# Cross-attention: queries spread for four heads, maxima turned in a batch's banks, half batches between fourths of the projections

## What is computed

```python
x = x + _L0_xattn_ref(_layernorm(x), ctx_1024, ...)
...
q = split_heads(x_q @ Wq + bq) * dp_scale
k = split_heads(x_kv @ Wk + bk)
v = split_heads(x_kv @ Wv + bv)
attn = jnp.einsum('bhic,bhjc->bhij', q, k)
neg = -jnp.finfo(attn.dtype).max
attn = jnp.where(causal_mask, neg, attn)
attn = jax.nn.softmax(attn, axis=-1)
o = jnp.einsum('bhij,bhjc->bhic', attn, v)
```

## Time and profile before

| | us |
|---|---|
| runs (3) | 1687.93, 1688.18, 1692.31 |
| median | 1688.18 |
| the profiled execution | 1688.73 |
| its span, first to last instruction | 1686.9 |
| TensorE busy | 1578.0 |
| VectorE busy | 1045.9 |
| ScalarE busy | 964.8 |
| GpSimd busy | 697.7 |

### The profile page before, as it was taken

How to read it: one execution, slowest core, us unless ns; L and a number is a source line. 1 busy time by engine, 2 the same in 40 slices (tenths; PEclk the granted TensorE clock), 3 DMA queues, 4 the chain that set the end, 5 groups by cost and what they waited for, 6 DMA issues and landing times. The chain is left out here.

```text
span 1686.9 us, 48994 instructions
## 1 busy us (share of the span) xinstructions
PE 1578.0 (94%) x20162; PEld 1362.0 (81%) x20179; DVE 1045.9 (62%) x1445; ACT 964.8 (57%) x1848; POOL 697.7 (41%) x627
## 2 busy tenths in 40 slices
PE   6999999999887999999999987998799999999988
PEld 5888888888666889888898765986588898898863
DVE  7667777786346877777777343045676666666622
ACT  4677777777413466656656712352367777777742
POOL 5655555551004655554554000000375555555202
PEclk9999999999977999999999999999999999999998
DMA  7665555554234766555555352971475555555430
GB/s 180 166 198 131 120 140 131 132 123 106 65 116 116 183 182 170 143 145 138 137 147 126 88 207 85 362 256 51 127 175 140 138 128 120 140 133 132 100 108 4
DMA packets 149248, 235.65 MB, mean 140 GB/s; under 512 B 24200, under 2 KB 64516, under 8 KB 148100
## 3 DMA queue, kind: packets, MB, share of 16 engines
q1 hardware_dynamic: 141090, 225.29, 50.6%
q10 hardware_dynamic: 7938, 7.23, 1.7%
HBM read 107.26 MB, written 0.23 MB: 64 GB/s over the span
## 5 line engine op out<-in xcount | busy, mean ns | idle before, releaser
L1305 DVE TENSOR_REDUCE L_xattn_maxima<-L_xattn_ps 128x4 f32<-128x1024 f32 x588 | 691.6, 1219 | 327.3 <-PE L_xattn_ps L877 323.2
L1067 ACT ACTIVATE L_xattn_p_ring<-L_xattn_ps 128x512 f32<-128x512 f32 x1176 | 674.9, 599 | 340.8 <-PE L_xattn_ps L926 325.7
L926 PE MATMUL L_xattn_ps<-L_xattn_q_packed,L_xattn_k_packed 128*128 128x256 f32 x2352 | 452.1, 298 | 10.0 <-ACT L_xattn_p_ring L1067 5.0
L926 PEld LDWEIGHTS L_xattn_ps<-L_xattn_q_packed,L_xattn_k_packed 128*128 128x128 f32 x2352 | 335.3, 190 | 71.6 <-issue 35.9
L962 PE MATMUL L_xattn_ps<-L_xattn_p_ring,L_xattn_v_ring 128*17 128x128 f32 x9408 | 289.3, 273 | 1.0 <-ACT L_xattn_p_ring L1067 1.0
L962 PEld LDWEIGHTS L_xattn_ps<-L_xattn_p_ring,L_xattn_v_ring 128*17 128x17 f32 x9408 | 242.4, 97 | 23.6 <-ACT L_xattn_p_ring L1067 1.6
L845 PE MATMUL L_xattn_ps<-L_xattn_ctx_halves,L_xattn_w_halves 128*128 128x256 f32 x1764 | 260.9, 286 | 0.5 <-POOL L_xattn_ctx_halves L1224 0.4
L849 PE MATMUL L_xattn_ps<-L_xattn_w_halves,L_xattn_ctx_halves 128*128 128x256 f32 x1764 | 260.4, 286 | 0.0
L1239 POOL TENSOR_TENSOR L_xattn_k_ring<-L_xattn_k_full,consts 128x512 fp32r<-128x512 f32 x147 | 155.5, 1058 | 223.0 <-ACT L_xattn_k_full L1080 111.6
L1221 POOL TENSOR_TENSOR L_xattn_ctx_halves<-L_xattn_ctx_chunk,consts 128x512 fp32r<-128x512 f32 x129 | 134.4, 1042 | 263.1 <-DMA L_xattn_ctx_chunk<-in_ctx_chunks 178.9
L845 PEld LDWEIGHTS L_xattn_ps<-L_xattn_ctx_halves,L_xattn_w_halves 128*128 128x128 f32 x1764 | 233.3, 193 | 3.7 <-issue 1.8
(11 more groups left out here) (385 smaller groups left out, 1173.2 us busy)
## 6 DMA issues: line engine op xcount, KB each, us to landing
L_xattn_k_packed<-L_xattn_k_ring SPq DMA_DIRECT2D x588, 128.0 KB, 2.4
L_xattn_ctx_chunk<-in_ctx_chunks SPq DMA_DIRECT2D x147, 256.0 KB, 3.2
L_xattn_k_packed<-L_xattn_k_ring SPq DMA_DIRECT2D x588, 64.0 KB, 2.2
L_ffn_W<-in_experts_W SPq DMA_DIRECT2D x16, 1024.0 KB, 13.7
L_xattn_mask_chunk<-L_xattn_mask ACTq DMA_DIRECT2D x49, 128.0 KB, 3.0
weights<-in_pack_L_attn SPq DMA_DIRECT2D x10, 512.0 KB, 4.3
L_xattn_ctxT<-in_ctxT SPq DMA_DIRECT2D x5, 896.0 KB, 12.9
L_xattn_ctx<-in_ctx SPq DMA_DIRECT2D x5, 896.0 KB, 11.8
```

The lines of the kernel that those rows point to most:

```text
L926: last = pe.matmul(L.ps[:, bank, d * 2 * S:(d + 1) * 2 * S], self.k_packed[s][:, quarter, d, half * P:(half + 1) * P], q[:, 2 * pair:2 * p ...
L1067: act.activation(self.p[t % P_RING][:, 4 * quarter:4 * quarter + 4, :], L.ps[:, E_BANK[unit], :].rearrange("p (h n) -> p h n", n=S), ACT.Exp)\
L1305: dve.tensor_reduce(out[:, 4 * v:4 * v + 4], L.ps[:, M_BANK + 2 * v:M_BANK + 2 * v + 2, :] .rearrange("p b (k n) -> p (b k) n", k=2), AX_X ...
```

## The change

Three things change, all in `CrossAttention`.

1. `q_hi` and `q_pairs` hold four matrices instead of sixteen: for each half of the heads one that keeps the even and one that keeps the odd heads of width 16 (mask `pair16`). A strip of 32 rows still sees one head at a time. VectorE's two operations shrink from 1024 to 256 columns, ScalarE's low halves from 16 operations to 4 and its copy from 2048 to 512 columns. `pack_queries` reads from the smaller matrices; its number of transfers stays.
2. In steps 6 to 48 (`borrows`) the turned maxima go to bank 2 and the factors to bank 3, which belong to the batch of this step, once the first half of its first batch has been reduced. The second batch of the step waits until ScalarE has taken the factors. The units keep banks 0 and 1 for themselves. `pe_factor` moves three projection matmuls ahead, and on ScalarE `act_factor` goes ahead of the drain of the values.
3. In steps 1 to 4 each half of a batch stands before one fourth of the projections.

```diff
@@ -51,7 +51,7 @@
 QUANTIZED = "L0_ffn"
 PART = 1024
 CONSTS = [("identity", P), ("ones", P), ("causal", P), ("causal_T", P), ("rope_cos", S), ("rope_sin", S),
-          ("head16", 8), ("head32", 4), ("neg_half", 1), ("fill", P), ("turned", 1), ("turn_sign", 1)]
+          ("head16", 8), ("head32", 4), ("pair16", 2), ("neg_half", 1), ("fill", P), ("turned", 1), ("turn_sign", 1)]
 
 
 HELD_FOR = {"L0_attn": "L0_ffn", "L1_ffn": "L2_xattn"}
@@ -96,7 +96,7 @@
         "identity": np.eye(P), "ones": np.ones((P, P)), "fill": fill,
         "causal": np.where(p[None, :] > p[:, None], NEG, 0.0), "causal_T": np.where(p[:, None] > p[None, :], NEG, 0.0),
         "rope_cos": np.cos(angle), "rope_sin": np.sin(angle) * sign,
-        "head16": p[:, None] // 16 == np.arange(8)[None, :], "head32": p[:, None] // 32 == np.arange(4)[None, :],
+        "head16": p[:, None] // 16 == np.arange(8)[None, :], "pair16": p[:, None] // 16 % 2 == np.arange(2)[None, :], "head32": p[:, None] // 32 == np.arange(4)[None, :],
         "neg_half": np.full((P, 1), -0.5),
         "turned": (p % DH < 2)[:, None],
         "turn_sign": np.where(p % DH == 0, -1.0, np.where(p % DH == 1, 1.0, 0.0))[:, None],
@@ -574,11 +574,21 @@
     return 6 if step < NCHUNK else 8
 
 
+def borrows(step):
+
+    return LAG <= step < NCHUNK
+
+
 def e_order():
 
     at, bank, before, used = {}, [], [], {}
 
     def unit(key, step):
+        if key[0] != "scores" and borrows(step):
+            before.append(-1)
+            at[key] = len(at)
+            bank.append(M_BANK if key[0] == "turned" else M_BANK + 1)
+            return
         free = E_BANKS if step < NCHUNK else E_BANKS + (KV_BANK,) if step < NCHUNK + 2 else TAIL_BANKS
         b = min(free, key=lambda i: (used.get(i, -1), free.index(i)))
         before.append(used.get(b, -1))
@@ -614,7 +624,7 @@
         self.norm = NormRows(L, bank=ACC_BANK)
         sb = L.sb
         self.w_halves = [sb(f"w_halves{h}", [P, 2, DC, D], F32R) for h in range(2)]
-        self.q_hi = sb("q_hi", [P, H, S], F32R)
+        self.q_hi = sb("q_hi", [P, 2 * DC, S], F32R)
         self.q_packed = [sb(f"q_packed{c}", [P, H, S], F32R) for c in range(2)]
         self.ctx_chunk = [sb(f"ctx_chunk{c}", [P, DC, KEYS]) for c in range(3)]
         self.ctx_halves = [sb(f"ctx_halves{c}", [P, 2, DC, KEYS], F32R) for c in range(3)]
@@ -631,7 +641,7 @@
         self.stage_T = sb("stage_T", [P, S], F32R)
         self.factor = sb("factor", [P, 4 * S])
 
-        self.q_pairs = self.p_ring[:, 0:2, :, :]
+        self.q_pairs = self.p_ring[:, 0, :, :].rearrange("p (a h) n -> p a h n", h=2 * DC)[:, 0:2, :, :]
         flat = self.p[2].rearrange("p h n -> p (h n)")
         self.qT = flat[:, 0:DC * S].rearrange("p (c n) -> p c n", n=S)
         self.qT_halves = flat[:, DC * S:3 * DC * S].rearrange("p (a c n) -> p a c n", a=2, n=S)
@@ -731,10 +741,9 @@
             sp.wait_ge(L["q_lo_heads_ready"], DC)
             sp.wait_ge(L["q_copied"], 1)
         packed = self.q_packed[0][:, :, :].bitcast(F32)
-        sp.dma_start(heads(packed[0:32, :, :]), heads(self.q_pairs[own, 1, :, :])).then_inc(L["q_packed_ready"], 16)
-        sp.dma_start(heads(packed[32:96, :, :]), self.q_pairs[own, :, :, :]
-                     .rearrange("r a (c h) n -> r a c (h n)", c=DC)[:, :, :, 2 * quarter * S:(2 * quarter + 2) * S])\
-          .then_inc(L["q_packed_ready"], 16)
+        pairs = self.q_pairs[own, :, :, :].rearrange("r a (c k) n -> r a c (k n)", c=DC)
+        sp.dma_start(heads(packed[0:32, :, :]), pairs[:, 1, :, :]).then_inc(L["q_packed_ready"], 16)
+        sp.dma_start(heads(packed[32:96, :, :]), pairs).then_inc(L["q_packed_ready"], 16)
 
     def fill_queries(self, sp):
 
@@ -851,19 +860,24 @@
         if part % 2 and end == 6:
             last.then_inc(L["k_in_psum" if part == 1 else "v_in_psum"], 1)
 
-    def pe_batch(self, pe, step, d):
+    def pe_batch(self, pe, step, d, first=0, end=4):
 
         n = step - 1
         if not 0 <= n < NCHUNK:
             return
         L, batch, slot, bank = self.L, 2 * n + d, n % K_RING, self.L.ps[:, M_BANK:M_BANK + 4, :]
         cornered = self.causal and n == NCHUNK - 1
+        b = block_turned(step)
         pe.wait_ge(L["q_heads_ready"], d + 1)
-        if d == 0:
+        if d == 1 and b and borrows(step):
+            pe.wait_ge(L["e_drained"], E_AT["factor", b] + 1)
+        if d == 0 and first == 0:
             pe.wait_ge(L["k_hi_ready"], n + 1)
             if self.masked:
                 pe.wait_ge(L["fill_ready"], n + 1)
         for strips in ((0, 1), (2, 3)) if step < LAG else ((0, 1, 2, 3),):
+            if not first <= strips[0] < end:
+                continue
             if batch:
                 pe.wait_ge(L["batch_reduced"], 2 * (batch - 1) + strips[-1] // 2 + 1)
             if self.masked:
@@ -874,7 +888,7 @@
             for k in range(2):
                 for r in strips:
                     own = slice(32 * r, 32 * r + 32)
-                    last = pe.matmul(bank[:, r, k * KEYS:(k + 1) * KEYS], self.q_hi[own, 8 * d + 2 * r + k, :],
+                    last = pe.matmul(bank[:, r, k * KEYS:(k + 1) * KEYS], self.q_hi[own, 2 * d + k, :],
                                      self.k_ring[own, slot, 0, d, :], start=not self.masked, stop=not cornered,
                                      tile_position=(32 * r, 0), skip_group_check=True)
                     if k and r % 2 and not cornered:
@@ -931,17 +945,23 @@
 
     def pe_turned(self, pe, b):
 
-        L, unit = self.L, E_AT["turned", b]
+        L, unit, step = self.L, E_AT["turned", b], turn_step(b)
         pe.wait_ge(L["stage_ready"], b + 1)
-        self.pe_bank_free(pe, unit)
+        if borrows(step):
+            pe.wait_ge(L["batch_reduced"], 4 * (step - 1) + 1)
+        else:
+            self.pe_bank_free(pe, unit)
         pe.transpose(L.ps[0:64, E_BANK[unit], 0:S], self.stage[:, :], self.net.const("identity"))\
           .then_inc(L["e_filled"], 1)
 
     def pe_factor(self, pe, b):
 
-        L, unit = self.L, E_AT["factor", b]
+        L, unit, step = self.L, E_AT["factor", b], turn_step(b)
         pe.wait_ge(L["e_drained"], E_AT["turned", b] + 1)
-        self.pe_bank_free(pe, unit)
+        if borrows(step):
+            pe.wait_ge(L["batch_reduced"], 4 * (step - 1) + 1)
+        else:
+            self.pe_bank_free(pe, unit)
         for i in range(4):
             last = pe.matmul(L.ps[:, E_BANK[unit], i * S:(i + 1) * S],
                              self.net.spread[:, 4 * i:4 * i + 4, :].rearrange("p h n -> p (h n)"),
@@ -981,12 +1001,9 @@
                 pe.wait_ge(L["q_packed_ready"], 16 * (9 if self.masked else 8))
                 pe.wait_ge(L["v_ones_ready"], 1)
             if step < LAG - 1:
-                self.pe_batch(pe, step, 0)
-                self.pe_project(pe, step, 0)
-                self.pe_project(pe, step, 1)
-                self.pe_batch(pe, step, 1)
-                self.pe_project(pe, step, 2)
-                self.pe_project(pe, step, 3)
+                for part in range(4):
+                    self.pe_batch(pe, step, part // 2, part % 2 * 2, part % 2 * 2 + 2)
+                    self.pe_project(pe, step, part)
             elif step == LAG - 1:
                 self.pe_project(pe, step, 0)
                 self.pe_project(pe, step, 1)
@@ -1013,9 +1030,10 @@
                 if b is not None:
                     self.pe_turned(pe, b)
                 self.pe_unit(pe, m, 5)
-                self.pe_project(pe, step, 3)
+                self.pe_project(pe, step, 3, 0, 3)
                 if b:
                     self.pe_factor(pe, b)
+                self.pe_project(pe, step, 3, 3, 6)
                 self.pe_unit(pe, m, 6)
                 self.pe_batch(pe, step, 1)
                 self.pe_unit(pe, m, 7)
@@ -1149,9 +1167,9 @@
 
         L = self.L
         act.wait_ge(L["q_lo_ready"], 1)
-        for h in range(HPB):
-            last = act.activation(self.q_pairs[:, 0, c * HPB + h, :], self.qT_halves[:, 1, c, :], ACT.Copy,
-                                  scale=self.net.const("head16")[:, h:h + 1])
+        for k in range(2):
+            last = act.activation(self.q_pairs[:, 0, 2 * c + k, :], self.qT_halves[:, 1, c, :], ACT.Copy,
+                                  scale=self.net.const("pair16")[:, k:k + 1])
         last.then_inc(L["q_lo_heads_ready"], 1)
 
     def act_copy_queries(self, act):
@@ -1189,12 +1207,14 @@
             for u in range(3, 9):
                 if u == turned_before(step) and b is not None:
                     self.act_turned(act, b)
-                if u == factor_before(step) and b:
+                if u == factor_before(step) and b and not borrows(step):
                     self.act_factor(act, b)
                 if u < 8:
                     self.act_unit(act, m, u)
                 if self.masked and u == 3 and 2 <= step + 2 < NCHUNK:
                     self.load_mask(act, step + 2)
+                if u == 5 and b and borrows(step):
```

(5 more changed lines are left out.)

## The result

The changed kernel takes 1682.5 us (median of 6 runs, 1678.5 to 1684.3); the kernel before takes 1688.1 (6 runs, 1685.8 to 1693.2). The ratio is 0.9962, with a 95% interval of 0.9944 to 0.9981: 0.4% or 5.6 us faster, where 14.7 had been forecast. The profiled execution took 1682.00 (span 1680.2 against 1686.9). The direction is right, the size is under half of the forecast, and the time lies above the range.

What follows compares the result with a forecast made beforehand. TensorE, busy 94%, was taken as the bound, standing still only in block steps and each layer's first five steps. Block steps 9.8 plus start-up 4.9 made 14.7 us off 1688.18: 1673.5 us, range 1666 to 1680.

Steps and rivals of the forecast that it cites:

- The first layer's start: First layer, first batch to last reduction of step 4: TensorE done at 38.9, reduced at 39.3, 3.2 us gained (1.5 to 5).
- Block steps: One step in four, 30 in all: own banks remove TensorE's waits, 0.39 less each (masked 0.26), 9.8 us gained (8 to 11.5).
- a tie: Block steps: first half reduction ends about 76.95, TensorE reaches the transpose at 76.96; 0.05 for about 12 steps, 0.6 us.
- The 5.32 of the third layer: Early step in the kernel before (1222.38 to 1227.70); against 5.3 with halves, interleaving by itself was to give nothing there.
- steps of 5.3 and 6.3: Early steps with half batches between fourths: 5.3 us on TensorE, 6.3 in the masked layer, with TensorE as the bound.
- VectorE's gaps of 0.84 and 0.70: Early steps: idle gaps before VectorE's four reductions (4.62 us), to be closed by an earlier keys' drain thanks to shorter queries.
- My quarter of 1.33: A quarter of an early step on TensorE: half batch 0.43 plus a group of six projections 0.90, 1.33 us.
- both parts (4.9): Start-up of the three layers, from smaller queries and half batches together: 3.2, 0.6 and 1.1, 4.9 us gained.
- The queries: First layer: VectorE's shrunken query operations bring the first reduction 1.4 us earlier (0.5 to 3.1); by size alone 3.1 freed.
- The masked layer: Masked layer's start: first batch 1 us earlier, at 531.7, steps of 6.3; 0.6 us gained (-2.5 to 2.5).
- The start-up gives nothing: Rival, layer starts: clock falls after TensorE's pauses, each costing 2 to 3 us; the 4.9 lost, 1678 to 1680; chance 0.18.
- The slower rival: Rival, block steps: one more hold of a shift operation by GpSimd in all 30, 20 us, 1693; chance 0.05.

Runs made afterwards that it cites:

- the load earlier: Changed kernel with the context's loads put one step earlier in SyncE's program: 1678.6 us, 0.9927 of the kernel before.
- parts 1 and 2: Changed kernel without half batches between fourths of the projections, so smaller queries and borrowed banks only: 1680.3 us, 0.9934 of the kernel before.
- the run with halves in step 1 alone: Kernel before with half batches between fourths of the projections in step 1 only, whole batches in steps 2 to 4: 1.0008 of the kernel before.
- part 1 alone: Kernel before with only the queries for four heads (smaller q_hi and q_pairs, with masks and packing): 0.9971 of the kernel before.
- part 3 alone: Kernel before with only the half batches between fourths of the projections, in steps 1 to 4: 1.0170 of the kernel before.

## Why the prediction was off

- **The first layer's start: the step that failed most.** The prediction summed TensorE's work from 20.4 ("half a step (2.6) to do and three steps (15.9): 38.9") as if nothing but VectorE's first reduction could hold it up, and put the shift's first operation at 39.3. It started at 43.76: the context's load stood behind the packing of the keys, TensorE paused 2.34 us, and the clock was low for 6.8 behind it. With the load earlier it started at 38.55. So the first layer lost 1.2 where 3.2 was forecast, and the queue's order is 4.2 of these 4.4. I looked at SyncE's queue for the packing of the queries and found it in time; I did not look at what stands in it behind the packing of the keys.
- **Block steps: mechanism right, size off.** 6.3 us measured, 9.8 summed. Three terms: the handoff from ScalarE's exponential to the batch, 0.10 where I wrote 0.05, with an exponential that ended 0.02 later (0.07 in each unmasked block step and 0.06 in each masked one, 2.0 in all); the transpose's wait, which I called a tie worth 0.6 in all and which is 1.2 (14 steps, 0.04 to 0.14 each); and the steps behind the block steps, which I left out and which are 0.02 to 0.10 longer in the unmasked layers (7.92 to 8.01 for 7.90 to 7.92), 0.8 in all. The error in the second is that I let TensorE go on as the reduction ended: from VectorE's end to the transpose 0.15 us pass. Where the reduction ended less than that before the transpose in the old trace, the tie became a wait.
- **The 5.32 of the third layer was the wrong thing to compare with.** This step failed too: it does not explain the miss of the sum, whose steps of 5.3 and 6.3 came, but it is why the third part looked free. I set a step of halves (5.3, measured 5.35) against a step of the kernel before (5.32) and found it neutral. But the first part closes VectorE's gaps of 0.84 and 0.70, as I wrote under it, and whole batches then take 5.02. Part 3's price is the difference to *that*: 0.33 in a step and 0.50 in a masked one, as far as TensorE is the bound. Over the whole starts it is 3.4, 0.5 and 0.9 (the change against parts 1 and 2): in the masked start TensorE waits 2.2 with halves and 4.6 with whole batches, so most of the price comes back there. My quarter of 1.33 was exact (1.34), and so was 6.3. The first part is what gained: its starts alone fell by 5.2 us together, more than I gave to both parts (4.9).
- **The queries.** The first reduction came at 17.93, 2.5 us earlier (I took 1.4), since two short operations took 1.71 in place of 4.17. The bound from the size was the nearer one. By the exclusive lock that the Trainium skill states ("SBUF — State Buffer", section on the two separate sides) I would have taken less. It did not decide: in the runs with part 1 alone and with parts 1 and 2 the same two operations took 2.8, and the reductions began at 17.24 and 17.62 all the same.
- **The masked layer, in part luck.** It gained 2.5 where 0.6 was forecast, and that hid a part of the miss. Its first batch comes 1.8 us earlier in the layer and not 1.0. And the trace before has a low stretch of the clock of 6.8 us in its steps 1 and 2 that the trace after does not have, which the prediction did not count; the run with halves in step 1 alone lacks it too, and its masked start is 37.3 without the first part.
- **The rivals.** "The start-up gives nothing" had named a fall of the clock once TensorE is the bound, though not this pause; but it kept the whole 9.8 of the block steps. What came is a part of each: 2.0 of 4.9 at the start, 6.3 of 9.8 in the block steps.
- **Steps 6 and the rest.** In the masked layer step 6 took 7.55 and not 6.81: VectorE's mask row was held to 1.35 us, and TensorE waited 0.77 for the maxima. That took 0.7 us back (another 0.2 is the third layer's, where a low stretch of the clock reaches into step 6):

```profile
564.57 1.35 DVE L1372 TENSOR_SCALAR L_xattn_fill_rows<-L_xattn_mask_chunk 128x256 fp32r<-128x256 f32 x1
```

```profile
568.34 0.51 PE L886 MATMUL L_xattn_ps<-L_xattn_fill_rows,L_xattn_fill_terms 2*128 2x512 f32 x4 [0.77 <-DVE L_xattn_maxima L1325]
```

  Another 0.7 is outside the three layers' steps; the granted clock's low stretches lie elsewhere in each execution, and no run here separates that from chance.
- **The slower rival** (one more hold of the shift in all block steps) did not come. The shift's last operation is held (0.90 to 1.07 us in place of 0.17) in 14 of the 20 unmasked block steps and in none of the masked layer's; in the old trace it was 11 and none, so not the two thirds of 30 that I wrote. In three other runs with borrowed banks it is 8 to 10, so the bank change does not bring more of them as a rule.

Not settled: why steps of halves can keep the clock down, and why they do so in one execution and not in another. That they can is what part 3 alone shows against the kernel before.

## What to carry to other kernels

When a change has parts, price each against the kernel that has the other parts, not against the trace of before: here one part closed the gaps that the other was meant to close, and the second was left with its cost alone. When a stage gets faster, walk every in-order queue that feeds it (a load behind a burst of transfers, a drain behind that load) and ask at which pace each still arrives in time. And where two instructions end within a tenth of a microsecond in a trace, count the handoff: a tie is a wait.

## What the runs showed of the hardware

- The same matmuls in another order kept the granted clock at 1.2 GHz for 34 and 41 us, with TensorE busy 30.00 of 30.00 us; with whole batches behind the same pause it rose after 6.8. In the changed kernel it rose after 6.8 amid the new order too, so the order can hold the clock down and need not. Where it does, that makes an order that costs 0.3 us in a step at 2.4 GHz cost 1.7% of the program.
- Handoffs, as the timelines have them, from the end of one engine's operation to the start of the matmul that waits for it: VectorE to TensorE 0.15 us, ScalarE or GpSimd to TensorE 0.10. A half batch of row-tiled matmuls between full ones costs 0.43 and lengthens the two groups of projections beside it by 0.1 each (six matmuls 0.91, where six inside a group of twelve take 0.72).
- A small operation of VectorE (128x16) takes 0.17 us as a rule. Where one took longer (0.68 to 1.17; 19 times in the changed kernel's trace, 16 in that of the kernel before), it ended 0.03 behind the end of an operation of GpSimd each time. Three of them in one block step made it 1.6 us longer.
